# Attention on VectorE: the reciprocals of the row sums, the row statistics and the row moments each issued one step later in the batch

## The reference

```python
h = tok(x)                                    # strided convolution and a normalisation: h is (32, 188, 256)
y = layernorm(h)
q, k, v = y @ W_q, y @ W_k, y @ W_v
latent = (k + v) @ W_down_kv                  # folded into the weights by the kernel
k_rec, v_rec = latent @ W_up_k, latent @ W_up_v
scores = q k_rec^T / 16 * exp(-0.01 |i - j|)  # 16 heads of 16
h = h + softmax(scores) v_rec @ W_o
h = h + experts(layernorm(h))                 # shared expert, routing, 16 experts
```

## Time and profile before

| | |
|---|---|
| median of 3 runs | 1873.16 us (1870.95 to 1875.5) |
| the profiled execution | 1870.4 us |
| its span in the trace | 1868.6 us |
| busy: PE, DVE, ACT, POOL | 90%, 66%, 48%, 51% of the span |
| granted TensorE clock, mean | 0.956 of full |
| instructions | 46715 |

### The profile page before, as it was taken

One profiled execution on the slowest core, in us unless ns is written; L12 is line 12 of the kernel. 1 busy time (PEld: TensorE's weight loads), 2 busy tenths in 40 slices (PEclk: granted clock), 3 DMA queues, 4 the chain that ended last, 5 costly groups with the idle time before them and its releaser, 6 DMA issues.

```text
span 1868.6 us, 46715 instructions
## 1 busy us (share of the span) xinstructions
PE 1689.0 (90%) x15566; PEld 1232.2 (66%) x15566; DVE 1224.8 (66%) x3739; ACT 902.6 (48%) x1965; POOL 950.2 (51%) x945
## 2 busy tenths in 40 slices
PE   6874899999999999579999669999999999999997
PEld 5873566666666665357777537777777777777775
DVE  3883788888888888384778655555555555555551
ACT  4442566666666665244233634444444444444442
POOL 3771244444444443272224054666666666666665
PEclk9995999999999999789999779999999999999999
DMA  5522455555555555242010232333333334333322
GB/s 189 176 94 50 106 121 126 134 123 133 132 127 128 129 136 116 50 133 51 26 34 26 96 123 86 102 101 97 93 93 100 98 100 101 101 101 99 101 34 28
DMA packets 220234, 186.52 MB, mean 100 GB/s; under 512 B 165625, under 2 KB 200953, under 8 KB 214009
## 3 DMA queue, kind: packets, MB, share of 16 engines
q1 hardware_dynamic: 193272, 141.11, 28.2%
q0 software_dynamic: 26880, 44.36, 11.5%
HBM read 134.49 MB, written 50.44 MB: 99 GB/s over the span
## 4 chain that ended last, share of the span: by engine, by line
PE 70%; DVE 12%; issue 8%; POOL 4%; SPq 2%; ACT 2%; DMA 2%; DVEq 1%; POOLq 0%; ACTq 0%
PE psum L1678 26%; PE psum L1695 13%; PE psum L1542 6%; PE psum L1560 4%; DVE arena L1086 4%; DVE psum L1094 3%; PE psum L1441 3%; PE psum L1498 2%; PE psum L1395 2%; PE psum L1409 2%; PE psum L1463 2%; PE psum L1420 2%; POOL hidden L570 2%; POOL arena L575 1%; PE psum L1508 1%
## 5 line engine op out<-in xcount | busy, mean ns | idle before, releaser
L1678 PE MATMUL psum<-arena,hidden 128*128 128x376 f16 x3072 | 493.1, 323 | 0.9 <-DVE arena L1320 0.9
L634 POOL TENSOR_TENSOR arena<-arena 128x376 f16<-128x376 f32 x320 | 317.4, 994 | 343.9 <-ACT arena L727 342.5
L1678 PEld LDWEIGHTS psum<-arena,hidden 128*128 128x128 f16 x3072 | 301.0, 98 | 188.9 <-issue 1.6
L727 ACT ACTIVATE arena<-arena 128x376 f16<-128x376 f32 (+5 forms) x610 | 287.3, 474 | 54.0 <-DVE arena L1250 43.1
L1086 DVE CUSTOM_DVE_ANT_0 arena<-psum,constants 128x188 f32<-128x188 f32 x768 | 228.0, 345 | 106.8 <-PE psum L1395 105.4
L727 ACT ACTIVATE arena<-psum 128x188 f32<-128x188 f32 (+7 forms) x457 | 168.1, 398 | 257.6 <-PE psum L1658 74.9
L926 ACT ACTIVATE arena<-psum 128x376 f32<-128x376 f32 x256 | 123.7, 483 | 342.2 <-PE psum L1678 342.2
L1330 DVE SCALAR_TENSOR_TENSOR arena<-psum,arena 128x376 f32<-128x376 f32 x256 | 140.8, 550 | 189.3 <-ACT arena L926 187.8
L1695 PE MATMUL psum<-hidden,arena 128*128 128x256 f16 (+1 forms) x2304 | 256.6, 273 | 0.0
L1695 PEld LDWEIGHTS psum<-hidden,arena 128*128 128x128 f16 (+1 forms) x2304 | 229.8, 103 | 21.8
L776 ACT ACTIVATE arena<-psum 128x564 f32<-128x564 f32 x256 | 164.0, 641 | 98.6 <-PE psum L1409 97.0
(11 more groups left out here) (156 smaller groups left out, 2644.2 us busy)
## 6 DMA issues: line engine op xcount, KB each, us to landing
arena<-q_halves SPq DMA_DIRECT2D x384, 47.0 KB, 2.4
arena<-k_halves SPq DMA_DIRECT2D x384, 47.0 KB, 2.3
arena<-e_g SPq DMA_DIRECT2D x16, 1024.0 KB, 5.1
arena<-e_u SPq DMA_DIRECT2D x16, 1024.0 KB, 5.2
arena<-e_d SPq DMA_DIRECT2D x16, 1024.0 KB
arena<-x_t SPq DMA_DIRECT2D x32, 376.0 KB, 3.5
weighed<-arena POOLq DMA_DIRECT2D x32, 376.0 KB, 3.9
q_halves<-arena SPq DMA_DIRECT2D x32, 188.0 KB, 3.1
```

The costliest lines, as they stand in the source:

```text
L634: nc.gpsimd.tensor_tensor(dst, f, hi, ALU.subtract).then_inc(ready, 1)
L727: return nc.scalar.activation(dst, src, ACT.Copy, scale=scale)
L1678: last = mm(bank[2 * (s % 2) + i][:, 0:CHUNK], w_, a, start=n == 0, stop=n == 5)
```

## The change

In VectorE's batch, the reciprocals (`invert`) go from the end of step 3 to step 4, both row statistics go to step 5, and the aggregation of the moments goes from step 6 to step 7, directly in front of the copy that reads its result. `row_max` and `times_decay` stay first in every step. No instruction is added or removed, and no other engine's list is edited.

```diff
                     elif j == 3:
                         add_out(b - 2)
+                    elif j == 4:
                         invert(b - 1)
-                    elif j == 4:
+                    elif j == 5:
                         row_stats(b - 2, 0)
-                    elif j == 5:
                         row_stats(b - 2, 1)
                     elif j == 6:
                         low_max(b + 1, 1 - par)
+                    elif j == 7:
                         row_moments(b - 2)
-                    elif j == 7:
                         keep_moments(b - 2)
```

## The result

The changed kernel takes 1892.81 us in the median of 6 runs (1888.55 to 1897.65), the kernel before 1872.66 (6 runs). The ratio is 1.0101, with a 95% interval of 1.0083 to 1.0119: slower by 20 us, or 1%. The forecast was slower by 11.8 us, 1885.0, in a range of 1874 to 1893. The sign and the mechanism were right, and the size was 0.6 of what was measured: the median lies only 0.2 us inside the upper end of the range, so that the range held by luck as much as by its working.

A forecast was written before the change was run, and what follows sets the result against it. PE and DVE take turns setting the pace, with POOL's chain releasing y in about every second batch. 25 batches at +0.42 us (+10.5) plus +1.3 at the ends give +11.8: 1885.0 us, range 1874 to 1893.

The forecast's parts named there:

- Part 1: Reciprocal leaves DVE's step 3, shrinking PE's stall before `take_max` at step 5: alone, a gain up to 0.36 us per batch.
- the ring: Loop reciprocal, SP's DRAM write and reads back, POOL's divide, PE's next y, next reciprocal: 18.49 us against a 18.07 us period.
- Part 2: Reciprocal behind step 4's `times_decay` starts 1.42 us later, delaying SP's queue; the loop grows 0.42 us, +10.5 us over 25 batches.
- The k halves at step 0: SP's later k reads for PE's `turned_scores` in the next batch: costed at nothing, with about 1 us of cover.
- From SP's write to POOL's divide: Leg from writing the inverse sums to the divide after their read back: taken as a mean of 9.59 us.
- The ends: Batches outside the 25 counted periods: 0.8 us early, about 0.7 at attention's end, -0.2 between; +1.3 us together.
- Part 3: First row statistic moves from behind DVE's step 4 to behind step 5, beside the other: costs nothing.
- Part 4: Moments leave DVE's step 6 for step 7, before their copy: between 0.28 us gain and 0.1 us loss a batch.
- A: Rival: shortest write-to-divide times, so the reserve is eaten but nothing more; +3 us or less, 1873 to 1876; 0.13 with D.
- D: Rival: no effect, SP itself is so late that the reciprocal's time does not matter; 0.13 together with A.
- B: Rival: reads issued later land sooner, PE's shorter period counts; 17.5 us a batch, 14 us less, 1859; chance 0.10.
- C: Rival: slower still, write-to-divide 9.97 us or k halves late for step 0; 18.87 us a batch, +21 us, 1894; chance 0.15.

The follow-up runs named there:

- experiment 11: Kernel before with only the reciprocals moved to step 4, and the four reads of the inverse sums issued by POOL: 1867.41 us, ratio 0.9966.
- Experiment 2: Kernel before with only the reciprocals moved to step 4, statistics and moments unmoved: 1892.57 us, ratio 1.0098.
- experiment 3: Full change with the reciprocals another step later, in step 5: 1958.24 us, ratio 1.0468.
- 5: Full change with three of SP's six reads of k halves issued ahead of its wait for the reciprocals: 1876.03 us, ratio 0.9998.
- experiment 7: Full change with the four reads of the inverse sums issued by POOL, not SP: 1872.49 us, ratio 0.9984.
- experiment 10: Kernel of experiment 6 with both row statistics in step 5 and nothing else moved: 1868.88 us, ratio 0.9977.
- experiment 6: Kernel before with the four reads of the inverse sums issued by POOL between its subtractions, not by SP: 1871.47 us, ratio 0.9977.
- Experiment 12: Full change with SP's k write held until the four reads of the inverse sums have landed: 1923.69 us in one run.
- experiment 4: Full change with SP's write of the q halves moved behind the four reads of the inverse sums: 1913.08 us, ratio 1.0212.
- experiment 9: Kernel of experiment 6 with the moments alone moved to step 7, directly before their copy: 1878.96 us, ratio 1.0032.

## Why the prediction was right, point by point

- **Part 1, the reciprocal leaves step 3.** Right: PE's stall at step 5 is gone in the profile after, and where the ring is out of the way (experiment 11) half the periods are 17.6 to 17.8 us. The mean there is 17.95 against 18.05, so 0.10 of the 0.36 us is seen over all 25.
- **Part 2, the ring.** Right in mechanism and place. Experiment 2 makes the loss with this edit alone, 3 makes it grow with the delay, 5 and 7 take it away from the other end, and every y product stands 0.15 us behind POOL. The k halves at step 0 had their cover: PE has no wait for them from 300 to 700 us.
- **The mis-sized terms of the ring.** The period grew by 0.70 us, not 0.42: 17.5 us over 25 periods, not 10.5. "From SP's write to POOL's divide" was taken as 9.59 us and measured 9.85, since the reads land 3.07 us behind their last issue in place of 2.78 (means of the 25 periods; 3.04 and 2.79 over the first 24): 6.5 us. Two y products at the lower clock added 1.34 and 1.48, together 2.8 us, and y to reciprocal was otherwise 5.47 and not 5.45, +0.4. The other two legs were 0.11 us shorter, -2.7. So 10.5 + 6.5 + 2.8 + 0.4 - 2.7 = 17.5. The clock was not a term of the prediction at all.
- **The ends.** The third y came 0.6 us later (0.8 was forecast). From the 28th y to the last it was 65.5 us against 62.5, +3.1 where +0.5 was forecast. I had taken the ring there as shorter since SP writes no halves. But the 29th y came 19.59 us behind the 28th, where 17.87 was measured before: from SP's write to the divide it was 10.80 us, with 4.14 us for the six reads of k halves and 3.75 behind the last read's issue. This y had waited 2.13 us and ran at the lower clock, and the 30th came 18.38 us behind it in place of 16.57. Another 1.1 us of the profile's 22.3 lies behind attention, and no edit reaches there. So 0.6 + 17.5 + 3.1 + 1.1 = 22.3 us, against 0.8 + 10.5 + 0.5 = 11.8.
- **Part 3, the statistics.** Right: nothing (experiment 10 against 6).
- **Part 4, the moments.** Wrong in size and sign. I priced the copy's wait as one hop of 0.15 us and took the whole edit as between a gain of 0.28 and a loss of 0.1 us a batch. It is a loss of 0.37 us (18.42 against 18.05) where nothing covers it: the copy waits 0.26 us, and 0.49 us more follow in every second batch. The gain of 0.28 us at `take_max` did not come either, since the stall at step 0 stayed, against the sign that the prediction named. The text did say that whatever it is would be swallowed by the wait for y, and it was: the full change and experiment 2 have the ratios 1.0101 and 1.0098 and the periods 18.77 and 18.67, and 0.06 of this 0.10 is the second y at the lower clock.
- **The rivals.** A and D (the reserve hides the delay) are excluded by the interval. A's sum was off by its ends: a ring of 18.2 us gives 3.2 + 1.3 = 4.5 us, not 3 or less. B (faster) fell on its premise, since the reads landed later, not sooner; and experiment 7 shows that its gain of 14 us did not exist with these places of the moments. C was priced at +21 us from one longest row. Its ring of 18.87 us was nearer to the measured 18.77 than the forecast's 18.49, and its distance of 9.97 nearer to the mean of 9.85. But no k half came late, and its sum fits only since the ends, +1.3 in it too, came to 4.8: in part luck.
- **The skill's figure.** With the 2.1 us that the prediction takes from the Trainium skill ("DMA: Bandwidth & Descriptors", Anatomy of one DMA) for a transfer of this size, the change would by its estimate not have been slower. The trace has 3.07 us on SP's path, and 2.79 (2.32 to 3.70) where GpSimd issues the reads in experiment 6, and the trace decides.

Still open: why the reads land later when they are issued later. Experiment 12 leaves the k write behind them as a possible part of it. The lowest mean, 2.32 us, is that of experiment 4, where no q write is issued in front of them; but its batches are 19.4 us long and all transfers lie otherwise, so this is a hint and not shown. Open is also why PE's clock fell behind a wait of 1.79 us and not behind one of 2.85 (experiment 3).

## What to carry to other kernels

A short operation whose result another queue waits for is not priced by its engine's busy time: count what that queue does behind the wait, close the chain back to the operation, and compare the whole turn with the period. When a turn is too long, look for work of the queue that can go in front of the wait; here three DMA issues gave back the 20 us that a 0.43 us reciprocal had cost. Then check what each moved transfer was itself covering, as experiment 4 did not.

## What the runs showed of the hardware that was not expected

- A VectorE instruction right behind its producer on the same engine, with a wait between, leaves the engine idle for 0.26 us in experiment 9, and in every second batch the next instruction starts another 0.49 us late. The producers are of 0.23 us in total; 1.15 us pass (0.74 in the other batches) where 0.37 do with other work between.
- The half clock of PE is not given by the length of a wait alone. It was seen behind waits of 1.72, 1.79 and 2.13 us in the profile after, and a wait of 2.85 us in experiment 3 left it at full speed. In that run it fell behind waits of 2.04 to 3.21 us and held behind others of 2.08 to 3.23.
- POOL issues the four reads of 47 KB in 2.45 us, SP in 2.22; in the rows of experiment 6 the divide stands 2.53 us behind (412.55 - 407.57 - 2.45), and 2.79 in the mean of 25 periods, no later than with SP's (2.78 before).
